# Sending each token to its two experts only, through slots in DRAM, in a gated attention and mixture-of-experts kernel

## What is computed

```
x = x + tanh(g_xattn) * xattn(layernorm(x), ctx, ctx, mask)        # 16 heads of 64
xf = layernorm(x).reshape(8192, 128)
probs = softmax(xf @ Wg + bg)                                      # 8 experts
w, idx = top_k(probs, 2);  w = w / sum(w)
comb = sum(one_hot(idx, 8) * w[..., None], axis=1)
h = relu(einsum('nd,edh->enh', xf, W1) + b1)                       # 256 hidden, every expert
y = einsum('enh,ehd->end', h, W2) + b2
x = x + tanh(g_ffn) * einsum('end,ne->nd', y, comb)
```

## Time and profile before

| | us |
|---|---|
| median of 3 runs | 1107.59 (1106.73 to 1108.70) |
| the profiled execution | 1107.66 |
| its span in the trace | 1105.6 |
| busy PE, DVE, ACT, POOL | 1024.9, 894.4, 943.1, 791.7 |

### The profile page before, as it was taken

How to read it: one execution, slowest core, us unless ns; L and a number is a source line. 1 busy time by engine, 2 the same in 40 slices (tenths; PEclk the granted TensorE clock), 3 DMA queues, 4 the chain that set the end, 5 groups by cost and what they waited for, 6 DMA issues and landing times.

```text
span 1105.6 us, 36301 instructions
## 1 busy us (share of the span) xinstructions
PE 1024.9 (93%) x13797; PEld 755.4 (68%) x13797; DVE 894.4 (81%) x1803; ACT 943.1 (85%) x1809; POOL 791.7 (72%) x719
## 2 busy tenths in 40 slices
PE   5868799999999999999999999999999999999887
PEld 4446567776777777677777767777776777777655
DVE  2686688897888889788888978888897888787766
ACT  3988788889898888989888898988889898887865
POOL 3566667776867777686777768777776877788843
PEclk9999899999999999999999999999999999999999
DMA  9122121212112121211212121121212111111100
GB/s 219 33 56 59 49 56 43 55 45 59 50 40 57 52 57 43 59 50 40 57 52 56 43 59 50 40 57 52 54 45 59 50 31 46 44 40 50 29 3 20
DMA packets 123162, 56.90 MB, mean 51 GB/s; under 512 B 26584, under 2 KB 122864, under 8 KB 122992
## 3 DMA queue, kind: packets, MB, share of 16 engines
q1 hardware_dynamic: 122992, 54.59, 19.3%
HBM read 16.80 MB, written 4.19 MB: 19 GB/s over the span
## 4 chain that ended last, share of the span: by engine, by line
PE 49%; DVE 14%; ACT 12%; issue 12%; POOL 11%; DMA 1%; ACTq 0%; DVEq 0%; SPq 0%; POOLq 0%
PE bank L44 15%; PE bank L46 14%; PE bank L45 14%; POOL hidL L895 3%; POOL ptL L932 3%; ACT qH L464 3%; POOL rstd L880 3%; PE bank L307 2%; ACT bank L520 2%; PE bank L262 2%; DVE shift L668 2%; ACT x2hat L508 1%; DVE comb L868 1%; ACT vH L559 1%; DVE above L844 1%
## 5 line engine op out<-in xcount | busy, mean ns | idle before, releaser
L895 POOL TENSOR_TENSOR hidL<-hid,hidH 128x512 f16<-128x512 f32 x242 | 278.6, 1164 | 21.3 <-ACT hidH L494 21.3
L932 POOL TENSOR_TENSOR ptL<-pt,ptH 128x512 f16<-128x512 f32 x128 | 148.5, 1160 | 179.4 <-ACT pt L579 179.4
L675 DVE TENSOR_TENSOR qL<-bank,qH 128x512 f16<-128x512 f32 x224 | 153.4, 685 | 57.1 <-ACT qH L464 53.7
L484 ACT ACTIVATE hid<-bank,b1col 128x512 f32<-128x512 f32 x256 | 185.6, 725 | 8.3 <-PE bank L46 8.2
L494 ACT ACTIVATE hidH<-bank,b1col 128x512 f16<-128x512 f32 x256 | 188.3, 736 | 0.0
L464 ACT ACTIVATE qH<-bank 128x512 f16<-128x512 f32 x256 | 155.1, 609 | 36.0 <-PE bank L46 35.0
L44 PE MATMUL bank<-w2H,hidH 128*128 128x128 f16 x1024 | 179.0, 220 | 5.8 <-DVE hidL L788 5.2
L46 PE MATMUL bank<-w2H,hidL 128*128 128x128 f16 x1024 | 179.1, 220 | 0.0
L45 PE MATMUL bank<-w2L,hidH 128*128 128x128 f16 x1024 | 179.1, 220 | 0.0
L927 POOL TENSOR_TENSOR x<-x,y_scaled 128x512 f32<-128x512 f32 x114 | 146.0, 1280 | 14.1 <-DVE x L746 14.1
L938 POOL TENSOR_TENSOR prob<-prob,row_inv 128x512 f32<-128x512 f32 x128 | 133.4, 1043 | 15.2 <-DVE row_inv L782 15.2
(11 more groups left out here) (143 smaller groups left out, 3607.3 us busy)
## 6 DMA issues: line engine op xcount, KB each, us to landing
vdH<-vH SPq DMA_DIRECT2D x256, 64.0 KB, 2.1
vdL<-vL SPq DMA_DIRECT2D x256, 64.0 KB, 2.1
x_raw<-in_x SPq DMA_DIRECT2D x16, 256.0 KB, 3.0
ctx_raw<-in_ctx SPq DMA_DIRECT2D x16, 256.0 KB, 3.1
mask_raw<-in_fside_Bx1xSxS SPq DMA_DIRECT2D x32, 128.0 KB, 2.8
out_x<-x SPq DMA_DIRECT2D x16, 256.0 KB, 2.5
qH<-in_L_xattn_Wq SPq DMA_DIRECT2D x1, 512.0 KB, 6.0
qH<-in_L_xattn_Wk SPq DMA_DIRECT2D x1, 512.0 KB, 8.1
```

The lines of the kernel that those rows point to most:

```text
L484: act.activation(hid[:, k % NR, :], bk("hid", g, e, c)[:, :], ACT.Relu, bias=b1col[:, e, c:c + 1]).then_inc(s_relu[c], 1)
L675: dve.tensor_tensor(qL[at], bk("Q", g, h)[:, :].rearrange("p (b q) -> p b q", b=GB), qH[at], ALU.subtract).then_inc(s_q_low[h % 2], 1)
L895: pool.tensor_tensor(hidL[:, m % 2, c, :], hid[:, k % NR, :], hidH[:, m % 2, c, :], ALU.subtract).then_inc(s_hid_low[c], 1)
L932: pool.tensor_tensor(ptL[:, b % 2, :], pt[:, b % 2, :], ptH[:, b % 2, :], ALU.subtract).then_inc(s_pt_low, 1)
```

## The change

The dense experts are replaced. Tokens of up to three groups form a chunk (`CHUNKS` = 3, 3, 3, 3, 2, 1, 1 groups). For each group:

1. Routing gives each token two experts, two weights, and now also two slot numbers: its rank among the tokens of that expert in the chunk, counted by small matmuls against triangles of ones (`positions`), plus the expert's base.
2. POOL scatters the rows of `x2hat` to these slots in DRAM, 8 indirect transfers for a group (`scatter`, two in each of the steps i = 3 to 6). SP puts the residual `x2` into DRAM too.
3. At a chunk's end DVE computes a list of 128-slot tiles with their expert and first slot (`tiles_listed`, 11 small instructions on one partition).
4. Tiles are taken in pairs. The number of pairs is fixed in the program, 4 for each group of the chunk and 4 more: 92 in all, at `PAIR_STEP`. They stand at two in three steps for steps 40 to 111, and at every step from 112 to 155. SP loads a pair two steps ahead (`load_pair`: two times 128 rows from slots, two times an expert's packed weights, 128 x 642 fp32, from DRAM), with addresses read from the list by a register load before each transfer; PE turns the rows, 12 and 12 matmuls of 128 columns follow in the next two steps, DVE makes `y_rows` three steps after the pair's, and SP stores the two tiles over their slots (`store_pair`), again with register loads.
5. POOL gathers both rows of a token (`gather`, two for each 128 tokens), DVE adds them with their weights to the residual that SP has brought back, and SP stores the output. The combine steps run up to 163.

The steps now end at 166. Before the pairs begin, SP also clears the slots (44 transfers of 512 KB in steps 0 to 43). The expert weights are split once and written to DRAM. `STAGED` is gone: all low halves of queries are made on DVE. The buffers of a pair: three for rows and weights (`NW`), two for `y_rows`.

The core of the diff:

```diff
+CHUNKS = (3, 3, 3, 3, 2, 1, 1)
+PAIRS = [k for k, m in enumerate(CHUNKS) for _ in range(4 * m + 4)]
+def pair_steps():
+    ready = [GB * (e + 2) for e in ENDS]
+    steps = []
+    for n, k in enumerate(PAIRS):
+        window = ready[k + 1] - ready[k] if k + 1 < len(ready) else 1
+        at = ready[k] + (n - FIRST_PAIR[k]) * window // PAIRS.count(k)
+        steps.append(max(at, steps[-1] + 1) if steps else at)
+    return steps
...
 PE, in each step
-                if within(eg, GROUPS):
-                    hidden(eg, ei, 0)
...
-                    hidden(eg, ei, 1)
...
-                    expert_out(hg, hi)
+                if pair_at(s) is not None:
+                    turn_slots(pair_at(s))
...
+                if pair_at(s - 1) is not None:
+                    hidden(pair_at(s - 1))
...
+                if pair_at(s - 2) is not None:
+                    expert_out(pair_at(s - 2))
...
 DVE
-                if within(g + 1, GROUPS) and (g + 1, 2 * i) not in STAGED:
+                if within(g + 1, GROUPS):
                     queries_low(g + 1, 2 * i)
...
+                if pair_at(s - 3) is not None:
+                    n = pair_at(s - 3)
+                    dve.wait_ge(s_y, n + 1)
+                    if n >= 2:
+                        dve.wait_ge(*pair_stored(n - 2))
+                    dve.scalar_tensor_tensor(y_rows[:, n % 2], bk("y", n)[:, 0:2 * D].rearrange("p (t d) -> p t d", t=2),
+                                             1.0 / WS, w_ring[:, n % NW, :, B2_AT:B2_AT + D], ALU.mult,
+                                             ALU.add).then_inc(s_y_out, 1)
...
+                if pair_at(s) is not None:
+                    n = pair_at(s)
+                    dve.wait_ge(s_slot_high, n + 1)
+                    dve.tensor_tensor(slot_xtL[:, n % 2, :], bk("slotT", n)[:, 0:2 * P], slot_xtH[:, n % 2, :],
+                                      ALU.subtract).then_inc(s_slot_low, 1)
...
 POOL
+                if 3 <= i < 3 + GT and within(g - 2, GROUPS):
+                    scatter(g - 2, i - 3, 0)
+                    scatter(g - 2, i - 3, 1)
+                if combine_at(s) is not None:
+                    gather(combine_at(s), 0)
+                    gather(combine_at(s), 1)
...
 SP
+            def listed(n, t, what, top):
+                k = PAIRS[n]
+                j = 2 * (n - FIRST_PAIR[k]) + t
+                return sp.value_load(tile_list[0:1, k % 3, what, j:j + 1], min_val=0, max_val=top)
+
+            def load_pair(n):
+                k = PAIRS[n]
...
+                if n >= NW:
+                    sp.wait_ge(s_y_out, n - NW + 1)
+                for t in range(2):
+                    at = listed(n, t, 0, ROWS[SLOTS_IN[k]] - P)
+                    sp.dma_start(slot_rows[:, n % NW, t, :], slots[SLOTS_IN[k]][bass.ds(at, P), :]).then_inc(s_rows_in[n % NW], 16)
+                    e = listed(n, t, 1, E - 1)
+                    sp.dma_start(w_ring[:, n % NW, t, :].unsqueeze(1),
+                                 w_dram[bass.ds(e, 1)].rearrange("e p f -> p e f")).then_inc(s_w_in[n % NW], 16)
+
+            def store_pair(n):
+                k = PAIRS[n]
+                sp.wait_ge(s_y_out, n + 1)
+                for t in range(2):
+                    at = listed(n, t, 0, ROWS[SLOTS_IN[k]] - P)
+                    sp.dma_start(slots[SLOTS_IN[k]][bass.ds(at, P), :], y_rows[:, n % 2, t, :]).then_inc(s_y_stored[n % 2], 16)
...
+                if pair_at(s - 3) is not None:
+                    store_pair(pair_at(s - 3))
+                if pair_at(s + 2) is not None:
+                    load_pair(pair_at(s + 2))
```

More of the change, by code:

```diff
@@ L107, in flamingo_block @@
         rank = sb("rank", [P, GT, E])
[L108 to L115, removed]
+        onehot = sb("onehot", [P, 2, GT, E])
@@ L120, in flamingo_block @@
+        hidH, hidL = (sb(f"hid{p}", [P, 2, 2 * HC * P], F16) for p in "HL")
+        x2_back = sb("x2_back", [P, 2, GT, D])
         q_bytes = [as_f32(q[:, :, :, :, :, :], "p a b c d e -> p (a b c d e)") for q in (qH, qL)]
@@ L346, in expert_out @@
[L346 to L358 removed]
+                if g == 0:
+                    pe.wait_ge(s_wdve, H // 4 + 5)
@@ new lines, in expert_out @@
+            def expert_out(n):
+                for freed in take_bank("y", n):
+                    pe.wait_ge(*freed)
+                pe.wait_ge(s_hid_low, n + 1)
+                for t in range(2):
+                    w2 = w_ring16[:, n % NW, t, :]
+                    for c in range(HC):
+                        at, cols = (t * HC + c) * P, c * D
+                        last = three_passes(pe, bk("y", n)[:, t * D:(t + 1) * D],
+                                            [h[:, n % 2, at:at + P] for h in (hidH, hidL)],
+                                            [w2[:, w + cols:w + cols + D] for w in (W2H_AT, W2L_AT)],
+                                            start=(c == 0), stop=(c == HC - 1))
@@ L400, in _ @@
                     queries(g + 1, 2 * i + 1)
+                if i == 0 and within(g - 2, GROUPS):
+                    route(g - 2)
+                if pair_at(s) is not None:
+                    turn_slots(pair_at(s))
                 if within(s, B):
@@ L736, in _ @@
                                              x_raw[:, rg % NX, ri, :], ALU.mult, ALU.add).then_inc(s_res, 1)
+                if ph == 7 and within(pg - 1, GROUPS):
+                    transposed_low("x2T", pg - 1, x2tL[:, :], x2tH[:, :], s_x2T_high, s_x2T_low)
                 if ph == 6 and within(pg + 2, GROUPS):
@@ L1024, in _ @@
                     load_x(g + 3)
-                yg, yi = (s - 2 - FFN_LAG) // GB, (s - 2 - FFN_LAG) % GB
-                if yi == 1 and within(yg - 1, GROUPS):
-                    store(yg - 1)
                 if within(s // 2, TILES):
```

792 lines of the change are left out of this document (451 added, 341 removed).

## The result

The changed kernel takes 1464.28 us (median of 4 runs, 1458.79 to 1471.30) against 1108.14 us for the kernel before (4 runs, 1106.73 to 1109.13). The ratio is 1.322, with a 95% interval of 1.316 to 1.328. The forecast was 1470 us in a range of 1240 to 1780. The profiled execution took 1466.2 us, with a span of 1464.1 us.

What follows compares the result with a forecast made beforehand. PE was taken to bound the kernel before, SP's queue and its rings the changed one. Start 47.7, then 267 + 588 + 252 + 286 and 29 for the end gave 1470 us, range 1240 to 1780.

Steps and rivals of the forecast that it cites:

- A: Steps 0 to 39, no pairs: 267 us in all, groups at 47, 52 and three of 56 us.
- the rings through SP's queue: Circular waits among SP's stores and loads and DVE's y_rows, once every step has a pair: 14.0 and 13.5 us.
- Stage B: SP's steps 40 to 109, two pairs in three steps: SP 8.2 us against DVE's 7.7, taken as 8.4, 588 us.
- The item of SP: One transfer with its register load on SP's queue: 0.6 issue, 0.6 load, 0.1 other register instructions, 1.3 us.
- Stage C: SP's steps 110 to 127, a pair in every step with attention: 18 steps of 14.0 us, 252 us.
- the second: Ring in which DVE's L923 waits for rows whose load was just issued: 13.5 us a step.
- Stage D: Last 26 pairs, after the attention: the ring stays, 11.0 us each, 286 us.
- the first ring: SP's load waits for y_out, which on DVE waits for a just-issued store to land: 14.0 us with attention.
- Slack on SP: Register loads cost next to nothing, rings are shorter, DVE bounds Stage B: 1273 us, chance 0.2.
- Heavy SP: Register load costs 1.2 us and more, SP bounds everything from step 40 on: about 1780 us, chance 0.22.
- Faster than before: SP and rings vanish behind the engines, DVE's step shrinks to 7.1 us: 1090 + 2 us, chance 0.05.
- The clock: PE's waits late in the kernel drop its clock to 1.2 GHz, adding 3.5 us a Stage C step: 1560, chance 0.13.

Runs made afterwards that it cites:

- c_noreg: Changed kernel with constants in place of its 552 register loads, so its output is wrong; 1369.0 us, ratio 1.236.
- f_floor: Changed kernel with third y_rows buffer, both row loads first, residual returned a step later, constants for all register loads (output wrong); 1206.6 us.
- e_reuse: Changed kernel with third y_rows buffer, both row loads first, residual returned a step later, stores reusing the loads' address registers; 1265.7 us.
- i_yhead: e_reuse with y_rows made at the head of DVE's step, ahead of residual, query and value work; 1224.8 us, ratio 1.105.
- j_nocombine: e_reuse without POOL's gathers and with DVE's two additions replaced by one-column copies, so output is incomplete; 1209.1 us.
- b_rowsfirst: Changed kernel with both row transfers issued first, SP waiting for y_rows only ahead of the weights; 1335.8 us, ratio 1.206.
- a_rows3: Changed kernel with three buffers for y_rows instead of two, so DVE waits for an older store; 1463.4 us, ratio 1.321.

## Why the prediction held

The time came within 0.4%, but several terms missed and their misses cancel. Against the spans of 1464.1 and 1470 us the start was 3 us and A 15 too high, B 4, C 2 and the rest 6 too low (step 127 taken as 15 us). The closeness of the number is luck; the direction and the rings through SP's queue are not.

**Before step 40**: 251.7 us instead of 267. DVE was the fullest engine as forecast, 223 of 251 us. Its work in a group was mis-sized, 45.1 and 45.8 us in the third and fourth where the sum had 43.3 + 9 = 52.3. The fourth:

```profile
188.60:239.20 50.60, 43.67 (x615) 31.29 (x614) 45.81 (x112) 37.98 (x77) 29.01 (x29) 0.93 0.55 161
```

By the distances between starts the new routing is 4.5 and 4.9 us of it, where 9 stood, and the rest 40.7 and 40.9, where 43.3 stood. Most of the small instructions take near 0.2 us where I allowed up to 1.0. `above` (line 752 now) does not have one price but two. Both kernels' lines, ns min, median, max:

```profile
L844 DVE TENSOR_TENSOR above<-logit x16: 426/976/1136, 148.8 to 1074.4; 128x256 f32<-128x256 f32 x16
```

```profile
L752 DVE TENSOR_TENSOR above<-logit x16: 424/425/1232, 140.3 to 1236.5; 128x256 f32<-128x256 f32 x16
```

Nine of the 16 in the changed kernel meet no POOL instruction and take 0.42 us. The other seven start within 0.45 us after POOL's line 1084 has started, and each ends 0.28 or 0.29 us after POOL's end, so that they take 0.89 to 1.23:

```profile
490.92 1.04 POOL L1084 TENSOR_TENSOR prob<-prob,row_inv 128x512 f32<-128x512 f32 x1
491.01 1.23 DVE L752 TENSOR_TENSOR above<-logit 128x256 f32<-128x256 f32 x1
```

For it the rule in the Trainium skill (SBUF — State Buffer, Who interferes with whom), that such an instruction contends with a GpSimd instruction reading SBUF, had been weighed to save some 4 us a group with a lighter POOL. The trace agrees with the rule: what decides is whether POOL is inside such an instruction at that moment. The first four `above`, up to 300 us, all met one (0.89 to 1.05 us); of the twelve behind them nine did not.

**Stage B**: 8.46 us a step for 8.4, the size right and the reason wrong. The step was summed as SP's queue, 8.2 us. SP was indeed nearly full (it waited some 30 us of 592, so its own work was 8.0 a step), but c_noreg and f_floor show that freeing it of all register loads brings 0.25 us. What set the step was DVE at 82% and its meetings with other queues. On e_reuse, with a B of 8.37, the bank that `y_rows` held was worth 0.37 us a step (i_yhead) and the combines 0.54 (j_nocombine). DVE's 7.7 as a floor was good: j_nocombine reached 7.83. How the rest of the step divides is not shown.

**The item of SP**: a transfer with its register load takes 1.11 us from one to the next (1207.32 and 1208.44, and on), 1.3 were forecast. The register load is 0.27 us with 0.15 for the arithmetic behind it, where 0.6 + 0.1 stood; the issue is 0.35 where 0.6 stood, as the row I took was that of a placement from SBUF to SBUF. About 0.25 us of gaps had no term. The ends of 0.05 and 1.2 us that made the range held the value.
The Trainium skill (DMA: Bandwidth & Descriptors, Latency and other measured facts) gives 600 ns as the floor of a tensor_load. The measured 262 to 272 ns, here from SBUF, are below it, and the measurement decides.

**Stage C**: 15.5 us a step from step 113 on for 14.0; steps 110 to 113 took 32.4 us together, before the rings had closed, and that hid the miss. That stages C and D are rings through SP's queue was the mechanism, and b_rowsfirst shows it. Which of the two stands in front was wrong: the second, put at 13.5, is the longer, and a_rows3 shows that the first costs nothing while the second stands. Its terms: 3.4 us to the third issue for 3.3, landing 2.6 for 3.0, and 8.7 from there to `y_rows`, where 0.7 + 5 + 1.5 = 7.2 were given to PE's turn, the rest of the step, and DVE. DVE waits 0.75 us for the store, and not 2.5. A part of the 8.7 is the clock: the grant was 0.50 from 1078.9 to 1082 us, and twelve of the pair's matmuls started 0.107 us apart, which is 0.6 us. The rest is not taken apart.

**Stage D**: 10.5 us a pair for 11.0. Three errors met. The 11.0 was the first ring; the plain turn is the second, 9.64 with items of 1.11. In it are 1.2 us of low clock, for which the sum had nothing. And every fourth pair SP waits for the output's landing at line 1141, on which the prediction had no word. It counted in SP's steps, which load two ahead, 18 steps and then 26 pairs; by DVE's steps, as here, 28 pairs stand in steps 128 to 155, and 28 x 10.5 and 27 for the end are the 321 us behind step 127, against 286 + 29.

**POOL's indirect transfers**: 1.0 us and a gap of 0.3, forecast 1.1. Two in a step left POOL at 60% of stage B, so it never bound.

**The rivals.** Slack on SP (register loads free, 1273 us) is refuted by c_noreg: 95 us hang on them. Heavy SP (1.2 us a load) by the row of 272 ns. Faster than before: neither of its two conditions was met, pairs of the last 44 at less than 6.4 us and a step of 7.1 in B; even i_yhead has 6.3 in D, but 9.8 in C and 8.0 in B. The clock fell as its rival said, and that is in the measured time; its price was put too high. In D it is 1.2 us a pair, where the rival had under 1; in C, where it had 3.5 a step, 0.6 us are shown. So the rival's mechanism was at work, at a part of its price.

## What to carry to other kernels

When the bounding engine is relieved, ask what the new work makes the in-order queues wait for. Here PE lost 64% of the experts' arithmetic; 240 of the 356 us lost came back by another order in two queues, one more buffer and two register loads less a pair, and the rest is a tail without other work to hide it. A transfer queued behind a wait that it doesn't need costs its latency in every turn. Count a ring through a queue term by term, but name both rings where they are near each other, since only the longer pays.
A sum that comes out right doesn't prove its terms. Here the forecast step of stage B and the real one agreed to 0.06 us with another cause.
A run that raises a mean tests nothing until the rows at the critical place are read: much of the high clock fell to the filling matmuls and the waits, and the matmuls in the ring mostly did not get it. In the same way one row of an instruction is not its price where another engine can be in its way.

## What the runs showed of the hardware

- A register load from SBUF on SP's queue takes 262 to 272 ns, and 1.11 us pass from one such load with its transfer to the next.
- The issue of a transfer on SP's queue has more than one price: a median of 346 ns for 128 rows from DRAM to SBUF, 607 for a placement of 64x2x256 from SBUF to SBUF (and the same after). Whether the shape or the memories make the difference is not shown.
- An indirect transfer of 128 rows occupies POOL for 0.96 to 1.0 us, with 0.3 of idle time behind it.
- The 128x256 `above` of two SBUF inputs takes 0.42 us on DVE, and 0.89 to 1.23 where it starts inside POOL's 1.04 us instruction of line 1084: it then ends 0.28 or 0.29 us after POOL's, seven times of seven.
- 24 matmuls of 128 columns start 0.107 us apart at a grant of 0.50 and 0.056 apart at 1.00. Filling matmuls raised the mean grant of a stretch from 0.59 to 0.80, but after a wait for rows of 2 to 9 us the pair's own matmuls mostly started 0.107 us apart again.
